# One decoder layer of state-space mixer, cross-attention and experts: a loop over ticks replaced by an unrolled list of due times

## The reference

```
x = layernorm(x + mixer(x))                 # mixer itself returns out + x
x = layernorm(x + cross_attention(x, ctx, ctx))
x = layernorm(x + experts(x))
```

## Time and profile before

| | |
|---|---|
| median of 3 runs | 1157.1 us (1156.52 to 1158.71) |
| the profiled execution | 1156.59 us, its span from first to last instruction 1154.8 us |
| mean granted clock of PE | 0.825 |

### The profile page before, as it was taken

One profiled execution on the slowest core, in us unless ns is written; L12 is line 12 of the kernel. 1 busy time (PEld: TensorE's weight loads), 2 busy tenths in 40 slices (PEclk: granted clock), 3 DMA queues, 4 the chain that ended last, 5 costly groups with the idle time before them and its releaser, 6 DMA issues.

```text
span 1154.8 us, 13667 instructions
## 1 busy us (share of the span) xinstructions
PE 898.6 (78%) x3960; PEld 681.7 (59%) x3960; DVE 793.7 (69%) x1239; ACT 501.0 (43%) x957; POOL 469.3 (41%) x281
## 2 busy tenths in 40 slices
PE   4934558947879998857789999577799975867995
PEld 2433446446658885356568875265588862645884
DVE  1699996568898957569989864599989751213333
ACT  3545451745434624645535516465445322312232
POOL 1259970074445731273627510654537413000222
PEclk9955557869679999779789999697789996756998
DMA  6136611110205431102025411112045412001451
GB/s 205 47 103 237 234 37 26 67 37 26 103 28 178 152 110 57 74 22 107 19 74 184 154 56 67 64 37 92 19 147 167 153 37 109 1 0 37 155 182 55
DMA packets 43439, 105.65 MB, mean 91 GB/s; under 512 B 4447, under 2 KB 13288, under 8 KB 43358
## 3 DMA queue, kind: packets, MB, share of 16 engines
q1 hardware_dynamic: 43358, 104.68, 26.6%
HBM read 88.73 MB, written 11.74 MB: 87 GB/s over the span
## 4 chain that ended last, share of the span: by engine, by line
PE 61%; DVE 12%; issue 10%; POOL 9%; ACT 5%; DVEq 0%; POOLq 0%; ACTq 0%
PE ps L928 17%; PE ps L908 11%; PE ps L778 9%; PE ps L857 5%; PE ps L896 4%; POOL dbu L563 4%; DVE hs L1105 4%; PE ps L851 2%; PE ps L952 2%; POOL parts L551 2%; PE ps L977 2%; PE ps L836 2%; POOL work L583 2%; DVE yacc L1155 1%; PE ps L960 1%
## 5 line engine op out<-in xcount | busy, mean ns | idle before, releaser
L563 POOL TENSOR_TENSOR dbu<-v,bbc 128x1024 f32<-128x1024 f32 x128 | 301.8, 2368 | 202.5 <-DVE v L1090 117.6
L1105 DVE TENSOR_TENSOR_SCAN hs<-ps,carry,dbu 128x512 f32<-128x512 f32 x256 | 317.1, 1269 | 2.6 <-issue 1.4
L674 ACT ACTIVATE ps<-delta,neg_a 128x512 f32<-128x512 f32 x256 | 176.2, 692 | 231.7 <-DVE hs L1105 231.5
L778 PE MATMUL ps<-ident,hs 128*128 128x128 f32 x1024 | 183.3, 337 | 98.4 <-DVE yacc L1155 83.5
L778 PEld LDWEIGHTS ps<-ident,hs 128*128 128x128 f32 x1024 | 154.8, 177 | 126.6 <-DVE hs L1105 76.8
L928 PE MATMUL ps<-x_hi,parts 128*128 128x512 f32 x576 | 181.4, 438 | 0.0
L596 POOL TENSOR_TENSOR work<-work,cbc 128x512 f32<-128x512 f32 x64 | 82.1, 1283 | 228.4 <-ACT work L766 228.4
L1155 DVE SCALAR_TENSOR_TENSOR yacc<-ps,ctok,yacc 128x512 f32<-128x512 f32 x240 | 167.3, 738 | 1.2 <-PE ps L778 1.0
L908 PE MATMUL ps<-w2s,work 128*128 128x256 f32 x576 | 136.8, 380 | 3.6 <-DVE work L1266 3.6
L908 PEld LDWEIGHTS ps<-w2s,work 128*128 128x128 f32 x576 | 108.2, 189 | 23.1 <-DVE work L1266 5.3
L928 PEld LDWEIGHTS ps<-x_hi,parts 128*128 128x128 f32 x576 | 109.7, 199 | 19.0 <-DVE work L1196 0.6
(11 more groups left out here) (165 smaller groups left out, 1093.6 us busy)
## 6 DMA issues: line engine op xcount, KB each, us to landing
parts<-parts_dram SPq DMA_DIRECT2D x72, 512.0 KB, 3.6
bbc<-brow_dram SPq DMA_DIRECT2D x32, 512.0 KB, 4.5
parts_dram<-parts SPq DMA_DIRECT2D x18, 512.0 KB, 4.0
w2s<-in_w SPq DMA_DIRECT2D x36, 256.0 KB, 4.0
cbc<-comb_dram SPq DMA_DIRECT2D x32, 256.0 KB, 3.6
w13s<-in_w SPq DMA_DIRECT2D x18, 256.0 KB, 3.1
work<-work SPq DMA_DIRECT2D x16, 256.0 KB, 2.3
xn<-in_x SPq DMA_DIRECT2D x5, 512.0 KB, 5.3
```

Source lines behind the costliest of these rows:

```text
L563: pool.tensor_tensor(dbu[:, i % DRING, :, :], v[:, 2 * h:2 * h + 2, :], bbc[:, n // 2 % 2, n % 2, :].rearrange("p (o t) -> p o t", o=1) .t ...
L674: act.activation(ps[:, unit % 2, :], delta[:, q, :], ACT.Exp, scale=neg_a[:, q * NS + m:q * NS + m + 1]).then_inc(da_done.sem, 1)
L778: last = pe.transpose(ps[:, bank, t * P:(t + 1) * P], src(t), ident[:, :])
L1105: dve.tensor_tensor_scan(hs[:, m % 2, q, 0:TC], ps[:, unit % 2, :], dbu[:, n % DRING, q % 2, :], carry[:, m, q:q + 1], ALU.mult, ALU.add). ...
```

## The change

The loop and the tick parts are gone. Each step has a due time in ticks of a scan part (32 ticks, two units each), in tables: `OWN` (chunk j itself), `BEFORE`, `TILE` and `EXPERT` (second stage of chunk j-1, y included), `AHEAD` (chunk j+1: x load to v). `period(j)` sorts all steps of a part by due time, and `streams` issues parts 0 to 4 one after the other for every engine, fully unrolled; chunk 0's `AHEAD` list runs first by itself. The last three sums of a chunk's states fall at the start of the next part. Buffers of u, delta and C are doubled, others share memory, and many waits are added for that.

Other edits: the state scans of the first chunk of a sequence start from a tile of zeros instead of a masked carry. Gates z are copied raw early in part j and get their silu at tick 14.7. Softplus is now max(y, 0) + ln(1 + exp(-|y|)): Abs and Relu on ACT from PSUM, Exp and Ln on tiles of 128 x 1024, the addition on POOL, and v on POOL too. Rope: a second key block with exchanged partitions is kept (`kblk[:, 1]`), the sin table is loaded exchanged, DVE makes q * cos and q * sin from PSUM, and each score is the sum of two matmuls. The setup of the keys moves into part 0 (tick 8.5). A tile of attention has one tick, and half experts start 0.95 tick apart.

```diff
+OWN = {"gates_in_0": 2.7, "gates_raw_0": 3.2, "gates_in_1": 4.5, "gates_raw_1": 5.0, "gates_silu": 14.7}
+BEFORE = {
+    "y_turn": 2.05, "y_skip_1": 2.65, "y_skip_0": 2.95, "y_gate_0": 3.45, "y_gate_1": 3.65,
+    "out_0": 3.7, "out_1": 4.1, "residual_0": 4.35, "residual_1": 4.66, "stats_x1": 4.95, "rstd_x1": 5.05,
+    "norm_x1": 5.4, "x1_turn": 5.7, "x1_keep": 5.9, "query_0": 6.1, "query_1": 6.3, "rope_0": 6.65, "rope_1": 6.95,
+    "stats_xl": 12.65, "rstd_xl": 12.66, "norm_xl": 12.7, "xl_turn": 12.8, "xl_keep": 12.9,
+    "ffn": 13.0, "relu_0": 13.45, "relu_1": 13.65, "stats_x2": 13.7, "rstd_x2": 13.8, "norm_x2": 14.0,
+    "x2_turn": 14.2, "x2_high": 14.4, "x2_low": 14.65, "w2_load": 14.66, "logits": 14.8, "top_two": 15.3, "score_exp": 15.35,
+    "combine": 15.65, "comb_turn": 15.7, "comb_keep": 15.8, "comb_store": 15.82, "out_bias": 16.8,
+    "experts_load": 12.5, "keys_load": 10.5, "rope_load": 1.7, "x1_load": 0.5,
+}
+TILE = {"score": 7.2, "maximum": 7.65, "soft": 7.7, "p_turn": 8.0, "p_keep": 8.1, "over": 8.15, "over_scale": 8.65,
+        "o_turn": 8.72, "o_keep": 8.76, "o_proj": 9.17, "attended": 9.6}
+TILE_STEP = 1.0
+GATE0, GATE_STEP = 15.8, 0.95
+EXPERT = {"a": 0.0, "gate": 0.01, "w2": 1.05, "second_load": 1.06, "b": 0.12, "half_load": 0.14, "weigh": 0.13,
+          "comb_load": 0.14, "product": 0.6, "hidden": 0.95}
+SUM, ROWS, SCAN, DECAY, SPREAD, BAND, CARRY = 0.0, 0.38, (0.4, 0.7), (0.41, 0.71), 0.42, 0.43, 0.9
+AHEAD = {
+    "x_load": 0.0, "squares": 1.5, "mean_sq": 1.9, "rms": 1.95, "x_scale": 3.0, "x_turn": 5.3, "x_keep": 5.6,
+    "edge": 10.0, "in_0": 11.8, "in_keep_0": 12.3, "conv_0": 12.95, "in_1": 13.4, "in_keep_1": 13.6, "conv_1": 14.1,
+    "edge_keep": 14.12, "conv_silu": 14.71, "xproj": 15.0, "rows_keep": 15.1, "rows_store": 15.11, "c_turn": 15.2,
+    "c_keep": 15.34, "dt_0": 15.4, "soft_in_0": 15.45, "dt_1": 15.75, "soft_in_1": 15.85, "dt_2": 16.1,
+    "soft_in_2": 16.15, "dt_3": 16.3, "soft_in_3": 16.35, "soft_exp": 16.7, "soft_ln": 16.9, "delta": 17.3,
+    "v_0": 28.5, "v_1": 29.5,
+}
+PREP_AT, PREP_STEP = 2.06, 1.0
+SETUP = {"setup_load": 0.01, "setup_zero": 0.02, "setup_work": 8.5, "setup_keys": 9.5}
+
+
+def numbered(name):
+
+    head, _, n = name.rpartition("_")
+    return (head, int(n)) if n.isdigit() else (name, 0)
+
+
+def period(j):
+
+    found = []
+    if 0 <= j < CHUNKS:
+        found += [(n + SUM, "sum", n - 3, j) for n in range(3, TICKS)]
+        found += [(n + ROWS, "rows", n - 2, j) for n in range(2, TICKS)]
+        found += [(u // 2 + SCAN[u % 2], "scan", u, j) for u in range(2 * TICKS)]
+        found += [(u // 2 - 1 + DECAY[u % 2], "decay", u, j) for u in range(2, 2 * TICKS)]
+        found += [(i - 2 + SPREAD, "spread", i, j) for i in range(2, TICKS)]
+        found += [(4 * k - 5 + BAND, "band", k, j) for k in range(2, NS // 2)]
+        if j % CPS != CPS - 1:
+            found += [(min(2 * m + 2, TICKS - 1) + CARRY, "carry", m, j) for m in range(NS)]
+        found += [(at, *numbered(name), j) for name, at in OWN.items()]
+    if j + 1 < CHUNKS:
+        found += [(TICKS - 1 + DECAY[u], "decay", u, j + 1) for u in range(2)]
+        found += [(TICKS - 2 + i + SPREAD, "spread", i, j + 1) for i in range(2)]
+        found += [(TICKS - 5 + 4 * k + BAND, "band", k, j + 1) for k in range(2)]
+    if 0 <= j - 1:
+        found += [(s + SUM - 0.01, "sum", TICKS + s - 3, j - 1) for s in range(3)]
+        found += [(s + ROWS - 0.01, "rows", TICKS + s - 2, j - 1) for s in range(2)]
+        found += [(at, *numbered(name), j - 1) for name, at in BEFORE.items()]
+        found += [(at + TILE_STEP * t, name, t, j - 1) for t in range(NT) for name, at in TILE.items()]
+        found += [(GATE0 + GATE_STEP * c + at, name, c, j - 1) for c in range(2 * ALL) for name, at in EXPERT.items()]
+        found += [(GATE0 + GATE_STEP * (2 * ALL + 1) + k / 100, name, 0, j - 1)
+                  for k, name in enumerate(("final", "rstd_xo", "norm_xo", "store"))]
+    if j + 1 < CHUNKS:
+        found += [(at, *numbered(name), j + 1) for name, at in AHEAD.items()]
+    if j == 0:
+        found += [(PREP_AT + PREP_STEP * c, "prepare", c, 0) for c in range(2 * ALL + PREP + 1)]
+        found += [(at, name, 0, 0) for name, at in SETUP.items()]
+    return [step[1:] for step in sorted(found, key=lambda step: step[0])]
...
+        def streams(step):
+
+            for name, at in sorted(AHEAD.items(), key=lambda item: item[1]):
+                step(0, *numbered(name), False)
+            for name in ("band", "spread", "decay"):
+                for n in range(2):
+                    step(0, name, n, False)
+            for j in range(CHUNKS + 1):
+                for name, n, chunk in period(j):
+                    step(chunk, name, n, j == CHUNKS)
...
+            def load_keys(seq):
+
+                sp.dma_start(kblk[:, 0, :], key_dram[seq]).then_inc(key_in.sem, 16)
+                for a in range(2):
+                    sp.dma_start(kblk[a:P:2, 1, :], key_dram[seq, 1 - a:P:2, :]).then_inc(key_in.sem, 16)
...
+                if name == "setup_load":
...
+                    sp.wait_ge(*delta_done.at(0, 2))
...
+                if name == "rope_load":
+                    sp.wait_ge(*rope_done.at(j, 0))
+                    sp.wait_ge(*sq_done.at(min(j + 2, CHUNKS - 1), 1))
+                    sp.dma_start(rope[:, 0, :], rope_q[j, 0]).then_inc(rope_in.sem, 16)
+                    for a in range(2):
+                        sp.dma_start(rope[a:P:2, 1, :], rope_q[j, 1, 1 - a:P:2, :]).then_inc(rope_in.sem, 16)
...
+                if name == "delta":
+                    for h in range(2):
+                        pool.wait_ge(*above_done.at(j, Q))
+                        pool.wait_ge(*ln_done.at(j, h + 1))
+                        d = deltas[j % 2][:, 2 * h:2 * h + 2, :]
+                        pool.tensor_tensor(d, above[:, 2 * h:2 * h + 2, :], d, ALU.add).then_inc(delta_done.sem, 1)
+                if name == "v":
+                    pool.wait_ge(*delta_done.at(j, n + 1))
+                    pool.wait_ge(*u_done.at(j, n + 1))
+                    pool.wait_ge(*dbu_done.at(j, n - 1))
+                    pool.tensor_tensor(v[:, 2 * n:2 * n + 2, :], deltas[j % 2][:, 2 * n:2 * n + 2, :],
+                                       us[j % 2][:, 2 * n:2 * n + 2, :], ALU.mult).then_inc(v_done.sem, 1)
...
+                if name == "gates_silu":
+                    act.wait_ge(*zraw_done.at(j, Q))
+                    for h in range(2):
+                        z = sz[:, 2 * h:2 * h + 2, :]
+                        act.activation(z, z, ACT.Silu).then_inc(sz_done.sem, 1)
+                    if j + 1 == CHUNKS:
+                        act.preload_act_table(ACT.Exp)
+                if name == "conv_silu":
+                    for h in range(2):
+                        act.wait_ge(*conv_done.at(j, (TAPS - 1) * 2 * (h + 1)))
+                        c = us[j % 2][:, 2 * h:2 * h + 2, :]
+                        act.activation(c, c, ACT.Silu).then_inc(u_done.sem, 1)
+                    act.preload_act_table(ACT.Exp)
...
+                if name == "soft_in":
...
+                    act.wait_ge(*dt_ps.at(j, n + 1))
+                    act.activation(deltas[j % 2][:, n, :], ps[:, 6 + n % 2, :], ACT.Abs, bias=col("dt_b", n)
+                                   ).then_inc(abs_done.sem, 1)
+                    act.activation(above[:, n, :], ps[:, 6 + n % 2, :], ACT.Relu, bias=col("dt_b", n)
+                                   ).then_inc(above_done.sem, 1)
+                if name == "soft_exp":
+                    for h in range(2):
+                        d = deltas[j % 2][:, 2 * h:2 * h + 2, :]
+                        act.wait_ge(*abs_done.at(j, 2 * h + 2))
+                        act.activation(d, d, ACT.Exp, scale=-1.0).then_inc(exp_done.sem, 1)
+                if name == "soft_ln":
+                    for h in range(2):
+                        d = deltas[j % 2][:, 2 * h:2 * h + 2, :]
+                        act.wait_ge(*exp_done.at(j, h + 1))
+                        act.activation(d, d, ACT.Ln, bias=1.0).then_inc(ln_done.sem, 1)
+                    act.preload_act_table(ACT.Exp)
...
+                if name == "gates_in":
+                    if n == 0:
+                        pe.wait_ge(*(yd_done.at(j - 1, 2) if j else above_done.at(0, Q)))
+                        pe.wait_ge(*xnt_done.at(j, KD))
+                    else:
+                        pe.wait_ge(*zraw_done.at(j, 2))
+                    for q in (2 * n, 2 * n + 1):
+                        input_block(Q + q, 6 + q % 2, z_ps)
...
+                if name == "c_turn":
+                    pe.wait_ge(*rows_done.at(j, 1))
+                    pe.wait_ge(*lg_done.at(j - 1, 0))
+                    transposes(6, lambda t: rows_t[:, t * P:(t + 1) * P], NT, ct_ps)
+                if name == "dt":
+                    pe.wait_ge(*(ctok_done.at(j, 1) if n == 0 else above_done.at(j, max(0, n - 1))))
```

(49 more changed lines are left out.)

1270 lines of the change are left out of this document (550 added, 720 removed).

## The result

The changed kernel takes 1360.1 us (median of 4 runs, 1355.6 to 1362.7) against 1156.8: ratio 1.175, 95% interval 1.172 to 1.179. The direction was forecast, the size was not: +203 us instead of +53, and 1360 lies outside the range of 1100 to 1265. The profiled execution took 1360.1 us, its span is 1357.9.

The account below looks back on a forecast made before the run. It took the second stage's serial chain of waits, not an engine's work, to bound the kernel: start 240 + parts 1 to 3 735 + tail 233 = 1208, plus 1.8 around it, 1210 us; 8 in 10: 1100 to 1265.

Parts of the forecast that it names:

- First scan: Start of the kernel: the first scan begins at 61 us, against 62.6 before.
- Part 0: First scan part, preparing chunk 1 under the scan: y of chunk 0 turned at 240 us, against 184.1.
- The chain of tables: ScalarE's silus and exponentials at tick 14.7, four table loads: DVE waits 13 us before the copy of C.
- The port: DVE operations with two SBUF inputs wait for running GpSimd operations: 6 us in part 0, 4 per period.
- The bare chain at full clock: Second stage in parts 1 to 3, each step right after the one before at full clock: 225 us.
- That rival (1282): PE falls to 1.2 GHz in attention: 24 us more a period, 1282 us in all; chance 0.14.
- the tail: Last chunk's second stage alone, from y turned to the end: 233 us, against 228.3 before.
- The preparation in a part: Next chunk's share of parts 1 and 2: x 2.2, in-projection 3.4, copy of C 6, convolution 4, port 3.
- Experts: Experts beside the scan in each period: 5.35 us a step, 17 steps 91, with final statistics 102.
- My signs for it: Trace signs expected in parts 1 to 3: scores 13 us apart, DVE idle half of it, released by PE's scores.
- The rival of queues that hide in the gaps (1137): DVE's work between hand-overs fills the chain's gaps: periods 231, 231, 225, total 1137 us; chance 0.29 faster.
- that of the scan (1040): The scan alone binds: 192 us a period, about 1040 us in all; chance 0.02 of the 0.29 for faster.

Follow-up runs that it names:

- e3: Changed kernel with both silus and the logarithm replaced by copies, so ScalarE loads no table inside a part: 1339.3 us, ratio 1.158.
- The filling: Changed kernel with identity transposes in PE's idle gaps, second try, those of a tile ahead of the previous tile's output turn: 1256.5 us, ratio 1.086.
- e14: The filling plus early x load, convolution at one column, no silus or logarithm, in- and x-projections of chunks 1 to 3 at 64 of 512 columns: 1194.5 us.
- e11: The filling with the convolution's 12 operations on DVE cut to one column each: 1242.9 us, ratio 1.078.
- e10: The filling plus early x load, silus next to each other, and ScalarE's second in-projection copies behind the normalising of x2: 1260.9 us, ratio 1.090.
- e15: As e10, with DVE's second half of the convolution behind its x2_low step, all work kept: 1259.3 us, ratio 1.090.
- e7: Changed kernel with each later state's sum on DVE cut to 128 of 512 columns: 1329.1 us, ratio 1.151.

## Why the prediction failed, step by step

- **First scan**: 61 forecast, 61.6. Right.
- **Part 0**: 240 forecast, 251.2. The chain of tables holds DVE 13.25 ahead of the copy of C (13 forecast); without the table loads (e3) 9.47 of it stays, so the loads are some 4 of it. DVE's waits by line:

```profile
97.19 2.16 DVE L1074 SCALAR_TENSOR_TENSOR work<-ps,vec,work 128x128 f32<-128x128 f32 x8 [4.88 <-PE ps L809]
...
109.67 0.76 DVE L1093 COPY vx<-ps 128x256 f32<-128x256 f32 x2 [6.94 <-PE ps L820]
...
126.96 8.83 DVE L1040 SCALAR_TENSOR_TENSOR u<-shared,vec,u 128x512 f32<-128x512 f32 x6 [0.17 <-ACT u L643]
...
169.02 0.23 DVE L1122 COPY ctok<-ps 128x64 f32<-128x64 f32 x1 [13.25 <-PE ps L781]
...
186.62 2.46 DVE L1150 TENSOR_TENSOR_SCAN hs<-ps,nothing,dbu 128x512 f32<-128x512 f32 x2 [3.38 <-ACT ps L699]
...
194.36 2.46 DVE L1150 TENSOR_TENSOR_SCAN hs<-ps,nothing,dbu 128x512 f32<-128x512 f32 x2 [3.98 <-POOL dbu L549]
```

  The setup's matmuls cost 11.8 (6 forecast) and the logarithm 7.4 (3); these two are most of the 11. The convolution with the port was 16.1 (8.83 here, 0.75 and 6.49 for the other half); 8.1 and a share of the port's 6 were forecast.
- **The port**: its direction holds. The convolution's operations, 0.742 to 0.753 in the kernel before, range from 0.727 to 2.843 now, at a median of 0.747. A few are held: one that started at 126.96 takes 2.42 and ends half a us behind a GpSimd product of 126.47 to 128.83. The y gate, which I had counted among them, is not: its sixteen take 0.667 to 0.691.
- **The bare chain at full clock: the step that failed.** "Each step right after the one before, at full clock" gave three tiles 39.9; with over, o_proj and the score at half clock they took 53.9, and 38.7 once the gaps were filled. From the last p_turn to the logits 30 was forecast, 33.4 with the in-projection; part 3 took 46.6 and part 1 55.4. Filled, part 3 takes 35.6 but part 1 still 52.5: there the preparation adds to the clock. I had both clocks in my rows: 0.55 in the drain with PE busy 62%, 0.77 in attention at 73%. I then took the full one and made the half clock a rival for the tiles alone. That rival (1282) was the right mechanism, priced at 72 us in the tiles of parts 1 to 3. The filling, which does not reach every gap, gives back 104. In the traces it is 96: 45 in those tiles, 17 in the tail's tiles, 29 from there to the logits, the rest in small pieces. 28 of it lie in the tail, whose forecast started from a drain that already ran at half clock and added 4 for half clock and long order together.
- **The preparation in a part: the second mis-sized term.** 19 forecast (in-projection 3.4, turn and copy of x 2.2, copy of C 6, convolution 4, port 3). Parts 1 and 2 are 42 to 44 longer than part 3 at filled gaps, some 4 of them y's earlier turn (4.5 and 3.1 in e14): about 39 measured. e11 to e14 show it as work of three engines on a chain with little slack; e10 and e15 that the queue places tried there do not free it. What e14 leaves, 16 to 19 with y's turn, stays unexplained.
- **Experts**: a step of 5.35 was forecast. In part 1 the products start 5.38 apart up to 496.5 and then 5.75 and 5.99 apart, it seems because the steps drift through the scan's ticks at 0.95 tick each:

```profile
491.13 0.69 DVE L1244 SCALAR_TENSOR_TENSOR work<-ps,work 128x512 f32<-128x512 f32 x1 [0.31 <-issue]
496.51 0.69 DVE L1244 SCALAR_TENSOR_TENSOR work<-ps,work 128x512 f32<-128x512 f32 x1 [0.36 <-issue]
502.26 0.67 DVE L1244 SCALAR_TENSOR_TENSOR work<-ps,work 128x512 f32<-128x512 f32 x1
508.25 0.67 DVE L1244 SCALAR_TENSOR_TENSOR work<-ps,work 128x512 f32<-128x512 f32 x1
```

  That they slow down is read from the trace; why was only argued. Part 3 slows down alike. What the preparation adds in part 1 is at the start: the first two steps take 8.75 and 10.83 there, 3.99 and 8.36 in part 3.
- **My signs for it**: tiles of 13 us with DVE idle half, released by PE's scores, were named as proof. DVE was so idle, 5.11 ahead of the maximum, but the tiles were 19: the sign that I wrote down for the right chain looked the same under the wrong clock. The rival of queues that hide in the gaps (1137) is refuted by the parts (266 to 302, where it needs 225 to 231), that of the scan (1040) by e7: with three quarters of the sums' columns gone the kernel takes 1329.

In the traces the miss is 150 of span (1358 for 1208). The filling gives back 96 of it. The other 53 are what the filled kernel still misses: part 0 11, parts 1 and 2 27 and 25, part 3 7, less 18 in the tail, which at full clock comes out shorter than forecast. Of the 27 and 25 some 20 each are the preparation (39 for 19). Clock and preparation are not quite apart: in parts 1 and 2 of the filled kernel the feed-forward still runs at half clock.
